# A cross-attention and mixture-of-experts layer on one core: a new order of loads, weight splits and transposes in its first and last stages

## The chip, the cores and the metric

The kernel runs on one NeuronCore of a Trainium2 chip, as one launch. The metric is the device time in microseconds (us) of that launch, median of several runs. A profiled execution gives a trace besides: start and duration of each instruction on the engines PE (TensorE, matrix products), DVE (VectorE), ACT (ScalarE), POOL (GpSimd) and SP (SyncE, which issues most DMAs).

## What is computed

Eight sequences of 112 rows, width 512, go through one layer:

```python
x = x + attention(layernorm(x), ctx)       # q, k_new, v_new = x wq, x wk, x wv
                                           # keys and values: [ctx (375 rows); x (112 rows)], softmax, times wo
x = x + ffn(layernorm(x))                  # 8 experts, the 2 best of each row, weights by softmax over the 2
# expert: y = (silu(x Wg) * (x Wu)) Wd, inner width 1024, everything float32
```

Every product of two float32 matrices is made of three products in a reduced format (fp32r): a = ah + al, b = bh + bl, and ab is taken as ah bh + ah bl + al bh. So each operand has a "hi" part, written by ACT (a copy into fp32r), and a "lo" part, written by DVE (the whole minus hi). PE needs both.

## The kernel before, in words

All engines run a program of their own, written out by hand; they meet only at semaphores, and on each engine the order of the code is the order of the work. The eight sequences go through attention in four pairs (A, B); then come the eight experts, each in eight units of 128 inner columns, in a loop over four pairs of experts.

Names: `x_all` the rows, `mr_all` their mean and 1/std, `xn` normalised rows, `T`, `PJ`, `SC`, `R` the PSUM banks, `xTh/xTl` transposed rows, `wTs/wTh/wTl` a weight as loaded, hi and lo (0 is wq, 1 wk, 2 wv, 3 wo), `qTh/kTh` and their lo parts, `kTs/vs` context keys and values, `vh/vl`, `vnh/vnl` values in parts, `ex` the exponentials, `aTh/aTl` these transposed, `on` the attention output, `oTh/oTl` that transposed, `xr` rows normalised for the experts, `ng` a loaded expert unit, `uh/ul` its parts, `eb` an expert's 256 gathered rows in parts, `gs/us/hs/hf/hh/hl` the hidden layer.

The start. SP issues x of the first two sequences, both halves of wq, x of the next two, then wk, wv, the contexts of pair 0, wo and the rest of x. DVE takes the statistics of a sequence (`stat_x`, `var_x`), POOL the power -0.5 of the variance, DVE normalises (`norm_x`), PE transposes (`pe_xT`), ACT and DVE split the result. Meanwhile ACT and DVE split the weights, in halves of 1024 elements a partition (`hi_w`, `lo_w`), and PE makes four projections (`pe_proj`: two for q, two for k, 24 products each). DVE also takes the statistics of sequences 2 and 3 and normalises them here, between the splits of wq and those of wk. While PE waits for the first data it runs products on the identity whose results nobody reads (`pe_idle`).

A pair (`body`). PE: `pe_vnew` A, `pe_scores` A, `pe_vnew` B, `pe_aT` A (transposes of `ex`), `pe_scores` B, transposes of the next pair's `xn`, `pe_attn` A (12 products), `pe_aT` B, then `pe_attn` B, `pe_oT` A and B, `pe_wo` A and B, with the projections of the next pair in between, and `pe_x2T`. In the last pair there is no next pair, and these stand next to each other. Each transpose is answered by ACT (hi) and DVE (lo) before PE can use it. The values' lo part (`vl`) is made by POOL, three instructions for each sequence (`lo_v`). SP waits for each stage and loads the next pair's contexts.

Towards the experts. SP loads four units in the last pair; ACT and DVE split the first three (`hi_u`, `lo_u` with u = 0, 1, 2). The rows of the first expert are gathered on PE: `pe_early` brings those of the first three pairs, read back from DRAM into `early`, and `pe_pick` those of the last pair. Between them PE runs transposes, logits, the `pe_prefix` products and idle products. `pe_gu_first` makes the first unit's two products; then the loop over units: `pe_gu` of the next unit, at two units of each expert (i == 3 and i == 6) the transposes of the next expert's rows (`pe_eT`, split by `hi_e` and `lo_e`), `pe_down` of the unit before. `pe_eT` for i == 6 waits for the lo part of the one before.

Of the kernel before, what the change touches and what calls it, by code (L numbers as in the profile page):

```python
# [40 lines left out]
def build_kernel(nc, x, ctxT, ctxn, w_all, gwt, units, out):  # L41
# [3 lines left out]
    with stack:  # L45
# [155 lines left out]
        w_hi, w_lo = sem("w_hi"), sem("w_lo")  # L201
        x_stat, x_rstd, x_norm = sem("x_stat"), sem("x_rstd"), sem("x_norm")
# [14 lines left out]
        total, most_ok = sem("total"), sem("most_ok")  # L217
# [6 lines left out]

        def hl_matmul(o, lh, ll, rh, rl, n):
            last = None
            for k in range(n):
                nc.tensor.matmul(o, lh(k), rh(k), start=k == 0, stop=False)  # L228
                nc.tensor.matmul(o, lh(k), rl(k), start=False, stop=False)  # L229
                last = nc.tensor.matmul(o, ll(k), rh(k), start=False, stop=k == n - 1)  # L230
            return last
# [12 lines left out]
        def pe_proj(c, bank):  # L244
# [25 lines left out]
        def pe_attn(pe, g, a, bank):  # L270
# [18 lines left out]
        def pe_wo(pe, g, a, bank):  # L289
            pe.wait_ge(o_lo, g + 1)  # L290
            hl_matmul(bank[0:S, :], lambda k: oTh[a][:, k, :], lambda k: oTl[a][:, k, :],
                      lambda k: wTh[3][:, k, :], lambda k: wTl[3][:, k, :], KT).then_inc(wo_mm, 1)
# [84 lines left out]
        def pe_gu_first(pe):  # L377

            pe.wait_ge(u_lo, 1)
            for w in range(2):  # L380
                for k in range(KT):
                    if w == 0 and k % 2 == 0:
                        pe.wait_ge(e_lo, k // 2 + 1)
                    c = slice(w * D + 128 * k, w * D + 128 * k + 128)
                    last = gu_product(GB[0][w], uh[0][:, c], ul[0][:, c], eb[0], k)
                last.then_inc(gu_mm if w else g_mm, 1)
# [30 lines left out]
        def pe_experts(pe, it, more=True):  # L417


            for u in range(1, UB + 1):  # L420
# [5 lines left out]
                if (i == 3 or i == 6) and (more or e == 0):  # L426
# [10 lines left out]
        def _(pe):  # L437
            pe.wait_ge(ident_ok, 1)
            pe_idle(R, 30)
# [3 lines left out]
            pe.wait_ge(x_lo, 2)  # L443
            pe.wait_ge(w_lo, 1)
            pe_proj(0, SC[0])
# [930 lines left out]
```

## Time and profile before

| | |
|---|---|
| three runs | 462.8, 463.65, 464.78 us (median 463.65) |
| the profiled execution | 463.22 us |
| its span, first to last instruction | 461.4 us |
| PE busy with products | 443.8 us, 96% of the span |
| DVE busy | 346.2 us, 75% |
| ACT busy | 251.7 us, 55% |
| POOL busy | 95.8 us, 21% |
| mean granted TensorE clock | 0.992 of full |
| share of PE in the chain that ended last | 89% |

PE is counted as busy when products run, useful or idle ones. The stage borders, in us from the span's start: the first projections 10 to 22, pair 0 until 67, pair 3 from 135 to 163, the way to the experts until 175, the experts until 452, and the last rows' way to DRAM until the end. Products are pipelined: a row's duration includes its latency, and products in a row start every 0.11 us (224 columns) or 0.23 us (512 columns).

### The profile page before, as it was taken

To read this page: it belongs to the slowest core of one execution; us is meant where nothing else is said; L and a number is where in the kernel's file an instruction comes from. 1 tells how busy PE (TensorE), PEld (TensorE's weight loads), DVE (VectorE), ACT (ScalarE), POOL (GpSimd) and SP (SyncE) were. 2 spreads that over 40 slices of the span, in tenths; PEclk is the share of its full clock that TensorE was granted. 3 is DMA by queue.
4 is the path that set the end of the run, shared out by engine and by line. 5 is a ranking of instruction groups with operands and counts; after the bars stand their busy time and mean duration, and the time that the engine had idled before them with its cause. 6 is when DMAs were issued, how large, how long until landed. Compare 5 with 4: busy or idle time off the path is not lost.

```text
span 461.4 us, 7183 instructions
## 1 busy us (share of the span) xinstructions
PE 443.8 (96%) x2549; PEld 376.0 (82%) x2549; DVE 346.2 (75%) x653; ACT 251.7 (55%) x409; POOL 95.8 (21%) x122
## 2 busy tenths in 40 slices
PE   8899999999999899999999999999999999999991
PEld 6878888888888578888888888888888888888870
DVE  5856646556644577998888888888888888888850
ACT  3648434524533536656656656656656656656621
POOL 4005071552425424003003003003003003003002
PEclk9999999999999999999999999999999999999996
DMA  8975994505544464955956946856856946856203
GB/s 237 396 229 150 290 238 138 167 23 145 195 137 189 123 224 115 344 199 200 268 172 194 277 167 200 270 166 202 269 168 200 276 161 220 264 160 201 40 1 51
DMA packets 26912, 88.40 MB, mean 192 GB/s; under 512 B 2560, under 2 KB 8704, under 8 KB 26880
## 3 DMA queue, kind: packets, MB, share of 16 engines
q1 hardware_dynamic: 23296, 80.13, 53.1%
q0 software_dynamic: 3584, 7.88, 8.3%
q8 instruction: 16, 0.26, 0.2%
q14 instruction: 16, 0.13, 0.1%
HBM read 73.55 MB, written 14.45 MB: 191 GB/s over the span
## 4 chain that ended last, share of the span: by engine, by line
PE 89%; DVE 4%; ACT 2%; POOL 1%; DMA 1%; issue 0%; POOLq 0%; SPq 0%; DVEq 0%; ACTq 0%
PE PJ L340 13%; PE T L340 13%; PE PJ L341 7%; PE T L341 7%; PE SC L228 4%; PE SC L230 4%; PE SC L229 4%; PE SC L413 3%; PE SC L412 3%; PE SC L411 3%; PE PJ L228 3%; PE PJ L230 3%; PE PJ L229 3%; PE T L236 3%; PE R L411 2%; PE R L412 2%
## 5 line engine op out<-in xcount | busy, mean ns | idle before, releaser
L750 DVE TENSOR_TENSOR ul<-ng,uh 128x1536 fp32r<-128x1536 f32 x64 | 112.5, 1758 | 3.1 <-ACT uh L536 2.1
L536 ACT ACTIVATE uh<-ng 128x1536 fp32r<-128x1536 f32 x64 | 94.6, 1480 | 0.0
L340 PE MATMUL PJ<-eb,uh 128*128 128x512 f32 x256 | 91.5, 397 | 0.1
L340 PE MATMUL T<-eb,uh 128*128 128x512 f32 x256 | 91.5, 397 | 0.0
L341 PE MATMUL PJ<-eb,ul 128*128 128x256 f32 x256 | 72.0, 281 | 0.0
L341 PE MATMUL T<-eb,ul 128*128 128x256 f32 x256 | 71.9, 281 | 0.0
L1170 POOL DMA_INDIRECT out<-ys,yidx x16 | 27.8, 1740 | 196.7 <-ACT ys L689 194.3
L340 PEld LDWEIGHTS PJ<-eb,uh 128*128 128x128 f32 x256 | 48.1, 188 | 11.7 <-issue 0.3
L340 PEld LDWEIGHTS T<-eb,uh 128*128 128x128 f32 x256 | 48.1, 188 | 11.5
L341 PEld LDWEIGHTS T<-eb,ul 128*128 128x128 f32 x256 | 48.3, 189 | 1.3
L341 PEld LDWEIGHTS PJ<-eb,ul 128*128 128x128 f32 x256 | 48.3, 189 | 1.3
L228 PE MATMUL SC<-xTh,wTh 128*128 128x224 f32 x128 | 36.0, 281 | 1.6 <-DVE wTl L750 1.0
L1108 POOL TENSOR_TENSOR vl<-vs,vh 128x512 fp32r<-128x512 f32 (+1 forms) x24 | 30.2, 1289 | 27.5 <-ACT vh L536 20.5
L229 PE MATMUL SC<-xTl,wTh 128*128 128x224 f32 x128 | 35.1, 274 | 0.0
L230 PE MATMUL SC<-xTh,wTl 128*128 128x224 f32 x128 | 35.1, 274 | 0.0
L536 ACT ACTIVATE us<-PJ 128x256 f32<-128x256 f32 x32 | 12.3, 384 | 32.6 <-PE PJ L341 32.6
L1013 DVE TENSOR_TENSOR hf<-us,hs 128x256 f32<-128x256 f32 x64 | 27.2, 425 | 2.9 <-ACT hs L699 0.9
L1015 DVE TENSOR_TENSOR hl<-hf,hh 128x256 fp32r<-128x256 f32 x64 | 27.2, 425 | 2.2
L536 ACT ACTIVATE us<-T 128x256 f32<-128x256 f32 x32 | 12.3, 384 | 30.0 <-PE T L341 30.0
L699 ACT ACTIVATE hs<-gs 128x256 f32<-128x256 f32 x64 | 26.3, 411 | 2.4 <-DVE gs L997 2.3
L228 PEld LDWEIGHTS SC<-xTh,wTh 128*128 128x128 f32 x128 | 24.6, 192 | 2.2 <-DVE wTl L750 1.2
L411 PE MATMUL SC<-uh,hh 128*128 128x512 f32 x64 | 25.8, 404 | 0.0
(206 smaller groups left out, 924.6 us busy)
## 6 DMA issues: line engine op xcount, KB each, us to landing
ng<-in_units SPq DMA_DIRECT2D x64, 768.0 KB, 4.3
vs<-in_ctxn SPq DMA_DIRECT2D x8, 768.0 KB, 4.9
kTs<-in_ctxT SPq DMA_DIRECT2D x8, 750.0 KB, 4.9
slots<-zero SPq DMA_DIRECT2D x8, 514.0 KB, 11.6
xe<-slots SPq DMA_DIRECT2D x8, 514.0 KB, 4.3
wTs<-in_weights SPq DMA_DIRECT2D x8, 512.0 KB, 9.4
out<-x_all SPq DMA_DIRECT2D x8, 224.0 KB, 3.7
x_all<-in_x SPq DMA_DIRECT2D x1, 896.0 KB, 18.0
```

What stands on the lines that cost most here:

```text
L228: nc.tensor.matmul(o, lh(k), rh(k), start=k == 0, stop=False)
L229: nc.tensor.matmul(o, lh(k), rl(k), start=False, stop=False)
L230: last = nc.tensor.matmul(o, ll(k), rh(k), start=False, stop=k == n - 1)
L340: nc.tensor.matmul(o[:, :].rearrange("p (h s) -> p h s", h=2), wh, both[:, k, :, :], start=k == 0, stop=False)
L341: return nc.tensor.matmul(o[:, 0:CAP], wl, both[:, k, 0, :], start=False, stop=k == KT - 1)
L411: nc.tensor.matmul(o, hh[b][:, s], wh, start=i == 0, stop=False)
L536: nc.scalar.activation(o, i, ACT.Copy).then_inc(s, 1)
L750: v.tensor_tensor(o, whole, hi.bitcast(F32), ALU.subtract).then_inc(s, 1)
L1013: link(v.tensor_tensor(hf[b][:, :], us[b][:, :], hs[b][:, :], ALU.mult))
L1015: v.tensor_tensor(hl[b][:, :], hf[b][:, :], hh[b][:, :].bitcast(F32), ALU.subtract)\
L1108: g_.tensor_tensor(vl[a][0:n, j, :], vs[a][0:n, j, :], vh[a][0:n, j, :].bitcast(F32), ALU.subtract).then_inc(v_lo, 1)
L1170: pool.indirect_dma_start(out[:, :], bass.IndirectOffsetOnAxis(yidx[:, e, t:t + 1], 0), ys[:, t, :], None, compute_op=ALU.add).then_inc(y_ ...
```

## The change

It has four groups of edits.

At the start: SP issues wk before x of sequences 2 and 3. The variance of each of the two first sequences goes to POOL by itself, and POOL takes two powers of one column in place of one of two. The first half of wq is split in two quarters, 512 elements a partition each (`hi_first_w`, `lo_first_w`), which ACT and DVE do after the split of the matching x; each half of the first projection waits for one quarter. All of wk is split before q is evicted. There is one idle product fewer (29).

In pair 0: statistics and normalising of sequences 2 and 3 now stand in the body, at the places that pairs 1 and 2 have for theirs. ACT copies `vh` of both sequences earlier.

In the last pair: the transposes of `ex` B come amid `pe_attn` A, those of `on` A amid `pe_attn` B, those of `on` B amid `pe_wo` A. ACT and DVE split `on` A's transposes before unit 0, and DVE makes `ul` of unit 1 only after the rows for the first expert.

Towards the experts: 15, 7 and 3 idle products in place of 12, 5 and 8; the two last sums of the counts come after `rows`; `pe_gu_first` opens its bank with a product on zeros and takes the `ul` products as soon as the hi part of the rows is there; the first transposes of the next expert come at i == 4 in place of i == 3; SP issues the loads of units 4 to 6 before those of the gathered rows `xe`.

The start on DVE, before (`wTl_102` is wq's lo part, `wTl_105` that of wk):

```order
L750 TENSOR_TENSOR wTl_102<-wTs_101,wTh_100 128x4x256
L750 TENSOR_TENSOR xTl<-T,xTh 128x4x112 x2
L750 TENSOR_TENSOR wTl_102<-wTs_101,wTh_100 128x4x256
L767 BN_STATS st<-x_all 112x6
L768 BN_AGGR mr_all<-st 112x2
L767 BN_STATS st<-x_all 112x6
L768 BN_AGGR mr_all<-st 112x2
L771 TENSOR_SCALAR ve_all<-mr_all 112x2
L777 TENSOR_SCALAR xn_146<-x_all,mr_all 112x512
L777 TENSOR_SCALAR xn_147<-x_all,mr_all 112x512
L750 TENSOR_TENSOR qTl<-SC,qTh 128x448
L750 TENSOR_TENSOR wTl_105<-wTs_104,wTh_103 128x4x256
```

and the same place after the change:

```order
L781 TENSOR_TENSOR xTl<-T,xTh 128x4x112
L781 TENSOR_TENSOR wTl_102<-wTs_101,wTh_100 128x4x128
L781 TENSOR_TENSOR xTl<-T,xTh 128x4x112
L781 TENSOR_TENSOR wTl_102<-wTs_101,wTh_100 128x4x128
L781 TENSOR_TENSOR wTl_102<-wTs_101,wTh_100 128x4x256
L781 TENSOR_TENSOR wTl_105<-wTs_104,wTh_103 128x4x256 x2
L781 TENSOR_TENSOR qTl<-SC,qTh 128x448
```

The seven instructions of statistics and normalising between wq and wk are gone from here, and both halves of wk stand before the first `qTl`.

The last pair on PE, before (`ex_131` is B's, `on_132` A's and `on_133` B's; the rows begin amid the twelve products of A and leave out what repeats up to B's seventh):

```order
L279 MATMUL PJ<-vh_124,aTh_136 112x512
L280 MATMUL PJ<-vl_122,aTh_136 112x512
L281 MATMUL PJ<-vh_124,aTl_138 112x512
L279 MATMUL PJ<-vh_124,aTh_136 112x512
L280 MATMUL PJ<-vl_122,aTh_136 112x512
L281 MATMUL PJ<-vh_124,aTl_138 112x512
L236 MATMUL T<-ident,ex_131 128x112 x4
L274 MATMUL PJ<-vnh_127,aTh_137 112x512
...
L281 MATMUL PJ<-vh_125,aTl_139 112x512
L236 MATMUL T<-ident,on_132 128x112 x4
L236 MATMUL T<-ident,on_133 128x112 x4
L228 MATMUL PJ<-wTh_109,oTh_140 112x512
```

and after:

```order
L285 MATMUL PJ<-vh_124,aTh_136 112x512
L240 MATMUL T<-ident,ex_131 128x112 x4
L288 MATMUL PJ<-vl_122,aTh_136 112x512
...
L285 MATMUL PJ<-vh_125,aTh_137 112x512
L240 MATMUL T<-ident,on_132 128x112 x4
L288 MATMUL PJ<-vl_123,aTh_137 112x512
...
L229 MATMUL PJ<-wTh_109,oTl_142 112x512
L240 MATMUL T<-ident,on_133 128x112 x4
L227 MATMUL PJ<-wTh_109,oTh_140 112x512
```

Each group of four transposes has moved ahead of five products (`ex` B, `on` A), or behind six (`on` B). The number of instructions is the same.

The lo parts in the last pair and towards the experts on DVE, before (`ul_169`, `ul_170`, `ul_171` are units 0, 1, 2):

```order
L750 TENSOR_TENSOR aTl_139<-T,aTh_137 128x448
L750 TENSOR_TENSOR ul_169<-ng_150,uh_161 128x1536
L750 TENSOR_TENSOR oTl_142<-T,oTh_140 128x448
L750 TENSOR_TENSOR oTl_143<-T,oTh_141 128x448
L750 TENSOR_TENSOR ul_170<-ng_151,uh_162 128x1536
L822 TENSOR_TENSOR x_all<-PJ,x_all 112x512
...
L1039 CAST mosti<-most 112x1
L750 TENSOR_TENSOR ul_171<-ng_152,uh_163 128x1536
L997 TENSOR_TENSOR gs_179<-PJ,gs_179 128x256
```

and after:

```order
L781 TENSOR_TENSOR aTl_139<-T,aTh_137 128x448
L781 TENSOR_TENSOR oTl_142<-T,oTh_140 128x448
L781 TENSOR_TENSOR ul_169<-ng_150,uh_161 128x1536
L781 TENSOR_TENSOR oTl_143<-T,oTh_141 128x448
L859 TENSOR_TENSOR x_all<-PJ,x_all 112x512
...
L1074 CAST mosti<-most 112x1
L781 TENSOR_TENSOR ul_170<-ng_151,uh_162 128x1536
L781 TENSOR_TENSOR ul_171<-ng_152,uh_163 128x1536
L1032 TENSOR_TENSOR gs_179<-PJ,gs_179 128x256
```

`oTl` of A has passed `ul` of unit 0, and `ul` of unit 1 has gone from ahead of the residual sum to right ahead of the first hidden layer's work.

The diff, cut to its core:

```diff
+                if pe:
+                    pe.wait_ge(first_lo, h + 1)
                 last = hl_matmul(bank[:, h * 2 * S:(h + 1) * 2 * S],
...
                 nc.tensor.matmul(o, aTh[a][0:n, j + 1, :], vh[a][0:n, j, :], start=False, stop=False)
+                if amid and j == 1:
+                    amid()
                 nc.tensor.matmul(o, aTh[a][0:n, j + 1, :], vl[a][0:n, j, :], start=False, stop=False)
...
+            for k in range(KT):
+                if amid and k == 2:
+                    amid()
...
             pe.wait_ge(u_lo, 1)
-            for w in range(2):
-                for k in range(KT):
-                    if w == 0 and k % 2 == 0:
-                        pe.wait_ge(e_lo, k // 2 + 1)
...
+            for h in range(2):
+                pe.wait_ge(e_hi, h + 1)
+                for k in (2 * h, 2 * h + 1):
+                    nc.tensor.matmul(GB[0][0][:, 0:CAP], ul[0][:, 128 * k:128 * k + 128], eh[0][:, k, :], start=False, stop=False)
+                pe.wait_ge(e_lo, h + 1)
...
-                if (i == 3 or i == 6) and (more or e == 0):
+                if (i == 4 or i == 6) and (more or e == 0):
...
+                    pe_attn(pe, A, 0, PJ[0], lambda: pe_aT(pe, B, 1, T[0]))
+                    pe_attn(pe, B, 1, PJ[1], lambda: pe_oT(pe, A, 0, T[1]))
+                    pe_wo(pe, A, 0, PJ[0], lambda: pe_oT(pe, B, 1, T[2]))
+                    pe_wo(pe, B, 1, PJ[1])
+                    pe_x2T(pe, A, 0, T[0])
+                    return
...
-            hi_w(0, 0)
             hi_x(0, 0, T[2])
+            hi_first_w(0)
             hi_x(1, 1, T[1])
+            hi_first_w(1)
             hi_w(0, 1)
+            hi_w(1, 0)
+            hi_w(1, 1)
             hi_pj(0, 0, SC[0])
-            hi_w(1, 0)
+            hi_w(2, 0)
...
                     hi_c(1, 1)
+                    hi_v(0, 0)
                 do_exp(A, 0)
...
                 hi_a(A, 0, T[0])
                 if p == 0:
-                    hi_v(0, 0)
+                    hi_v(1, 1)
...
-            g_.tensor_tensor(mr_all[:, 0:2, 1], ve_all[:, 0:2], half[0:S, 0:2], ALU.pow).then_inc(x_rstd, 1)
+            g_.tensor_tensor(mr_all[:, 0:1, 1], ve_all[:, 0:1], half[0:S, 0:1], ALU.pow).then_inc(x_rstd, 1)
+            pool.wait_ge(x_stat, 2)
+            g_.tensor_tensor(mr_all[:, 1:2, 1], ve_all[:, 1:2], half[0:S, 0:1], ALU.pow).then_inc(x_rstd, 1)
...
-            for h in range(2):
-                load_w(0, h)
-            sp.dma_start(x_all[:, 2:4, :], xv[:, 2:4, :]).then_inc(x_in[2], 16)
-            for n in range(1, 3):
+            for n in range(2):
                 for h in range(2):
                     load_w(n, h)
+            sp.dma_start(x_all[:, 2:4, :], xv[:, 2:4, :]).then_inc(x_in[2], 16)
...
-            load_ahead(0, range(2))
+            load_ahead(0, range(LG))
             sp.wait_ge(x2_out, 16 * NB + 16 * 2)
             for a in range(2):
                 sp.wait_ge(scattered[a], 32 * PAIRS)
-            load_xe(0, 0)
             sp.wait_ge(early_T, 1)
             load_xe(ER, 1)
-            load_ahead(0, range(2, LG))
+            load_xe(0, 0)
```

## Rows read from the trace of the kernel before

**Rows 1.** Busy time by stretch: us, then PE, PEld, DVE, ACT, POOL, clock, DMA, GB/s.
```profile
40.00:135.00 95.00, 95.00 (x627) 81.92 (x626) 57.33 (x129) 44.55 (x68) 34.13 (x38) 1.00 0.57 161
192.00:300.00 108.00, 108.00 (x578) 92.39 (x577) 96.79 (x167) 68.22 (x114) 10.85 (x9) 1.00 0.68 217
```

**Rows 2.** Timeline of PE, first projections: start, duration, instruction, [idle before it].
```profile
10.07 0.37 PE L228 MATMUL SC<-xTh,wTh 128*128 128x224 f32 x1 [0.54 <-DVE xTl L750]
...
16.74 0.37 PE L228 MATMUL SC<-xTh,wTh 128*128 128x224 f32 x1 [1.05 <-DVE wTl L750]
...
22.09 0.27 PE L230 MATMUL SC<-xTh,wTl 128*128 128x224 f32 x1
22.52 0.49 PE L228 MATMUL PJ<-wTh,xTh 128*112 128x512 f32 x1 [0.16 <-DVE wTl L750]
```

**Rows 3.** Timelines of ACT and of DVE in the same stretch.
```profile
7.98 0.98 ACT L536 ACTIVATE xTh<-T 128x448 fp32r<-128x448 f32 x2 [0.29 <-PE T L236]
...
14.01 1.00 DVE L777 TENSOR_SCALAR xn<-x_all,mr_all 112x512 f32<-112x512 f32 x2 [0.89 <-POOL mr_all L1113]
```

**Rows 4.** Timeline of PE, `pe_attn` of the first sequence.
```profile
37.38 0.48 PE L279 MATMUL PJ<-vh,aTh 119*112 119x512 f32 x1 [0.30 <-POOL vl L1108]
```

**Rows 5.** Timelines of POOL and DVE where both work; `kTl` subtractions: duration min/median/max.
```profile
38.17 3.79 POOL L1108 TENSOR_TENSOR vl<-vs,vh 128x512 fp32r<-128x512 f32 x3 [0.84 <-ACT vh L536]
...
41.25 2.29 DVE L750 TENSOR_TENSOR kTl<-kTs,kTh 128x1500 fp32r<-128x1500 f32 x1 [1.30 <-ACT kTh L536]
...
98.43 7.53 POOL L1108 TENSOR_TENSOR vl<-vs,vh 128x512 fp32r<-128x512 f32 x6 [2.35 <-DVE xr L832]
...
104.22 0.53 DVE L771 TENSOR_SCALAR ve_all<-mr_all 112x2 f32<-112x2 f32 x1
...
L750 DVE TENSOR_TENSOR kTl<-kTs,kTh x8: 1705/1722/2289, 22.6 to 122.1; 128x1500 fp32r<-128x1500 f32 x8
```

**Rows 6.** Timeline of PE, last pair.
```profile
150.52 0.55 PE L236 MATMUL T<-ident,ex 112*128 112x112 f32 x4
152.35 0.49 PE L274 MATMUL PJ<-vnh,aTh 112*112 112x512 f32 x1 [1.29 <-DVE aTl L750]
...
157.27 0.49 PE L228 MATMUL PJ<-wTh,oTh 128*112 128x512 f32 x1 [0.49 <-DVE oTl L750]
...
163.56 0.60 PE L236 MATMUL T<-ident,xr 112*128 112x112 f32 x4 [0.45 <-DVE xr L832]
```

**Rows 7.** Timelines of DVE and of ACT, last pair.
```profile
152.11 1.49 ACT L536 ACTIVATE uh<-ng 128x1536 fp32r<-128x1536 f32 x1
...
158.77 1.76 DVE L750 TENSOR_TENSOR ul<-ng,uh 128x1536 fp32r<-128x1536 f32 x1 [0.75 <-ACT uh L536]
160.44 0.69 DVE L822 TENSOR_TENSOR x_all<-PJ,x_all 112x512 f32<-112x512 f32 x1
```

**Rows 8.** The tile `early`: its load's issue (first and last start), its landing, its use.
```profile
L1256 SPq DMA_DIRECT2D early<-slots x1: 388/388/388, 158.7 to 158.7; - x1
...
DMA to landing us min/median/max: 3.7/3.7/3.7
...
164.62 2.05 PE L360 MATMUL SC<-ident,early 128*128 128x128 f32 x16
```

**Rows 9.** Timelines of DVE and of PE, first unit of the first expert.
```profile
175.95 1.75 DVE L750 TENSOR_TENSOR ul<-ng,uh 128x1536 fp32r<-128x1536 f32 x1
...
178.76 0.42 DVE L1011 TENSOR_TENSOR us<-PJ,us 128x256 f32<-128x256 f32 x1 [0.73 <-ACT us L536]
...
180.00 0.42 DVE L1015 TENSOR_TENSOR hl<-hf,hh 128x256 fp32r<-128x256 f32 x1
...
180.97 0.40 PE L411 MATMUL SC<-uh,hh 128*128 128x512 f32 x1
```

**Rows 10.** Timelines of PE and of DVE, first transposes of the next expert's rows.
```profile
189.39 0.60 PE L236 MATMUL R<-ident,xe 128*128 128x128 f32 x4
...
194.33 0.68 DVE L750 TENSOR_TENSOR eb<-R,eb 128x512 fp32r<-128x512 f32 x1
```

More of the change, by code:

```diff
@@ L227, in hl_matmul @@
             for k in range(n):
-                nc.tensor.matmul(o, lh(k), rh(k), start=k == 0, stop=False)
-                nc.tensor.matmul(o, lh(k), rl(k), start=False, stop=False)
-                last = nc.tensor.matmul(o, ll(k), rh(k), start=False, stop=k == n - 1)
+                last = hl_matmul_k(o, lh(k), ll(k), rh(k), rl(k), k, n)
             return last
@@ L379, in pe_gu_first @@
             pe.wait_ge(u_lo, 1)
-            for w in range(2):
-                for k in range(KT):
-                    if w == 0 and k % 2 == 0:
-                        pe.wait_ge(e_lo, k // 2 + 1)
-                    c = slice(w * D + 128 * k, w * D + 128 * k + 128)
-                    last = gu_product(GB[0][w], uh[0][:, c], ul[0][:, c], eb[0], k)
-                last.then_inc(gu_mm if w else g_mm, 1)
+            for h in range(2):
[3 more added lines that the diff above has]
+                pe.wait_ge(e_lo, h + 1)
+                for k in (2 * h, 2 * h + 1):
+                    last = nc.tensor.matmul(GB[0][0][:, :].rearrange("p (h s) -> p h s", h=2), uh[0][:, 128 * k:128 * k + 128],
+                                            eb[0][:, k, :, :], start=False, stop=k == KT - 1)
+            last.then_inc(g_mm, 1)
+            for k in range(KT):
+                c = slice(D + 128 * k, D + 128 * k + 128)
+                last = gu_product(GB[0][1], uh[0][:, c], ul[0][:, c], eb[0], k)
+            last.then_inc(gu_mm, 1)
         def pe_gu(pe, it, u):
@@ L478, in body @@
                     pe_xT(pe, A + 3, 1, T[1])
+                if not more:
+                    pe_attn(pe, A, 0, PJ[0], lambda: pe_aT(pe, B, 1, T[0]))
[4 more added lines that the diff above has]
+                    return
                 pe_attn(pe, A, 0, PJ[0])
                 pe_aT(pe, B, 1, T[0])
-                if more:
-                    pe.wait_ge(x_lo, A + 4)
-                    pe_proj(0, SC[0])
-                if p and more:
+                pe.wait_ge(x_lo, A + 4)
+                pe_proj(0, SC[0])
+                if p:
                     pe_prefix(pe, p - 1)
@@ L711, in experts @@
                         hi_u(it + 1, LG)
-                    if (i == 3 or i == 6) and (more or e == 0):
+                    if (i == 4 or i == 6) and (more or e == 0):
                         hi_e(2 * (2 * it + e + 1) + 1 + i // 6, (e + 1) % 2, i // 6, YB[(e + 1) % 2][i // 6])
@@ L851, in topk, with sums @@
                 dve.wait_ge(masked, p + 1)
+                if p < PAIRS - 1:
+                    sums(p)
+            def sums(p):
                 link(v.tensor_tensor(mnew[:, :], mboth[:, 0, :], mboth[:, 1, :], ALU.add))
@@ L931, in body @@
                     x2_norms(A - 1, 1)
-                if p and more:
-                    if p == 1:
-                        dve.wait_ge(x_in[3], 16)
+                if more:
+                    if p < 2:
+                        dve.wait_ge(x_in[2 + p], 16)
                     stat_x(A + 2)
@@ L939, in body @@
                 do_max(A, 0)
-                if p and more:
+                if more:
                     stat_x(A + 3)
@@ L947, in body @@
                 lo_a(A, 0, T[0])
-                if p and more:
+                if more:
                     norm_x(p + 1)
@@ L974, in body @@
                 lo_o(B, 1, T[2])
-                if not more:
-                    lo_u(0, 1)
                 x2_stats(A, 0, PJ[0])
@@ L990, in _ @@
             rows(PAIRS - 1)
+            sums(PAIRS - 1)
             lo_first(0)
@@ L1022, in experts @@
                         sum_g(it + 1, 0)
-                    if (i == 3 or i == 6) and (more or e == 0):
+                    if (i == 4 or i == 6) and (more or e == 0):
                         lo_e(2 * (2 * it + e + 1) + 1 + i // 6, (e + 1) % 2, i // 6, YB[(e + 1) % 2][i // 6])
@@ L1039, in _ @@
             v.tensor_copy(mosti[:, 0:1], most[:, 0:1]).then_inc(most_ok, 1)
-            for u in range(2, LG):
+            for u in range(1, LG):
                 lo_u(0, u)
```

105 lines of the change are left out of this document (55 added, 50 removed).

## The prediction

> **What bounds the kernel now.** I read the busy time by stretch first. From 40 to 135 us PE is busy for 95.00 of 95.00 us and from 192 to 300 for 108.00 of 108.00, at a granted clock of 1.00 [rows 1]. So in three quarters of the span nothing but fewer products could help, and the change takes none away there. What it can win lies where PE waits: the timeline of PE shows waits in the first projections [rows 2], once in the first sequence's attention [rows 4], and in the last pair [rows 6]. Time won in front of such a full stretch goes through it undiminished, since what follows waits for PE. The terms below are therefore differences in the time at which PE reaches a place, and they add.
>
> **The start.** Before, the first projection begins at 10.07 and the first product of `pe_vnew` at 22.52, 12.45 us for 96 products [rows 2]. The last 48 begin between 16.74 and 22.09, that is one each 0.114 us, a slow first one included. Without a gap 96 take about 10.8 us. The gap is 1.65 us, and the wait in it is for wk's lo part, which on DVE stood behind the statistics and the normalising of sequences 2 and 3, whose last piece is the row at 14.01 with 0.89 of idling ahead of it [rows 3]. After the change both halves of wk are split before `qTl`. My count of DVE from the split of x on: half a wq (1.2 us) and two of wk (2.3 us) are over at about 14.4, wanted at 15.8 and later; it holds as long as wk has landed by about 12, and its loads now stand ahead of a 448 KB load. I take the whole 1.65.
> Against it stands a later begin. The transposes are there at 7.98 and ACT splits the two x in 0.98 us [rows 3]. Now a quarter of wq stands between the two on ACT (0.6 us by my estimate, 512 elements against 448 in 0.5) and one on DVE (0.7); before, the first half of wq filled the time until 7.98 and was no burden. I get xTl at 10.25 in place of 10.0: 0.2 us lost (0 to 0.5). The earlier variance of x 0 buys nothing, as PE runs idle products until 7.3 anyway; the one dropped idle product gives 0.1, counted in. Net 1.45 us (bounds 0.8 to 1.8).
>
> **Pair 0.** PE waits 0.30 us at 37.38 for POOL's last piece of `vl`, with the slower restart 0.4 us [rows 4]. ACT's copy of `vh` moves ahead of the first exponential, where ACT idles, so POOL can begin earlier. But POOL's program has the power for sequences 2 and 3 first, and this now waits for DVE's statistics in the body. I put the begin of `vl` at 30.4 against 33.5; all three pieces at 34.2, wanted after 35. Gain 0.4 (0 to 0.5).
> The price: the normalising of sequences 2 and 3, at about 31.3 in the new time, now lies beside `vl` on POOL, which it did not in any pair before. The trace shows what such company does. A subtraction of two SBUF tensors that usually takes 1.72 took 2.29 when it began at 41.25 while POOL worked until 41.96; and the `ve_all` at 104.22, a two-element operation, took 0.53 and ended where the fifth of POOL's six pieces of 1.25 us (from 98.43) ends [rows 5]. DVE seems to be held until POOL's instruction in flight is over. For the two `xn` no row exists. Below: 0, if they slip in between. Above: each held a whole piece, so that the second ends about 1.1 us after PE wants its transpose at 32.9. I take one of them held for one piece, nearest to the row at 104.22: 0.6 us lost on PE (0 to 1.1).
> The Trainium skill, GPSIMD Engine Reference, section Specifications, says that GpSimd shares its SBUF interfaces with VectorE, with contention for instructions in a 2-port mode or with two SBUF inputs. The rows at 41.25 and 104.22 agree. By this rule the `xn` are exposed if they run in a 2-port mode, and the loss is in the upper half of the range; if they don't, it is 0 and the sum is better by 0.6.
>
> **The last pair.** In the old time scale. The transposes of `ex` B begin at 150.52 and the product that needs their lo part at 152.35: 1.83 us for transposes, ACT, DVE [rows 6]. They now begin five products of 0.233 us earlier, at 149.35 (the exponential is over at about 149.25, so with no reserve). The product starts at 151.2, 1.17 us earlier, 0.3 of it still a wait. `on` A's transposes come after seven of its twelve products, at 152.9, and with the same 1.83 us `pe_wo` A can begin at 154.7 in place of 157.27 [rows 6]. `on` B's transposes stand in the middle of it and cost it 0.4 us; they need ACT's scaling, which stands behind the copy of unit 0, an operation of 1.49 us [rows 7], and is done at about 156.0, where PE arrives at 156.15. `pe_wo` A ends 2.2 us earlier. On DVE the residual sum A began at 160.44, held by `ul` of unit 1 (158.77, 1.76 us) and not by PE [rows 7]; that `ul` is gone from there, and `ul` of unit 0 and `oTl` B are over at about 158.0. So sum, statistics and `x2T` A come 2.25 us earlier, at 161.3 in place of 163.56. I take 2.25 (bounds 1.6 to 2.5).
>
> **To the experts.** `early` is issued at 158.7 and takes 3.7, so it is there at 162.4; PE used it at 164.62 [rows 8], 2.2 us of slack. POOL's scatters ahead of it don't move with this pair's edits, so the slack is used up: PE arrives at 162.4 too. Besides, the store of `x_all` A is now issued beside it. I take 0.15 lost (0 to 0.7). The sums moved behind `rows` give 0.1; the idle products (25 after the last transposes before and after) only shift.
> `ul` of unit 1, one more operation like that at 175.95, now stands ahead of the first hidden layer: 1.67 us more on DVE. There, 0.73 us were idle at 178.76, and the chain ended at 180.42 with `pe_down` at 180.97 [rows 9]. I count `hl` ready at 181.42, so `pe_down` starts 0.5 us late (0.2 to 0.9). The `ul` products of unit 0 ahead of the wait for the lo part make PE about 0.24 us earlier at the unit's end, but only to wait longer for DVE: worth nothing. From then on DVE recovers, because it needs less than PE for a unit, and a backlog in the loop costs nothing. The move from i == 3 to i == 4 adds nothing to either engine.
>
> **The sum.** 1.45 + 0.4 - 0.6 + 2.25 - 0.15 + 0.1 - 0.5 = 2.95 us. The profiled execution took 463.22 us, a span of 461.4 and 1.8 around it; with the change 460.3. The median of the runs lies 0.43 higher, at 463.65: 460.7 us.
>
> **Rivals.** (1) The waits come back: the `xn` held for all of 1.1 us, `early` 0.7, `pe_down` 0.9, wk landing somewhat late. The sum falls by 1.45 to 1.5: 462.1. For it: three terms have no slack in my count, and a place where PE arrives just in time is usually late. Against it: each has been counted with durations of the trace. (2) The company on POOL does nothing and the start is not later: 2.95 + 0.6 + 0.3, time 459.8. For it: `ve_all` is a poor guide to a long operation. (3) Slower than before: the expert loop. `pe_eT` at i == 6 waits for the lo part of the transposes before, which now are two units ahead, not three. Before, transposes at 189.39 had their lo part at 195.01, 5.6 us [rows 10]. A unit lasts 4.2 us, so 8.4 are left. The point is 8.4 us from transposes to lo part; if the chain took 9.4, seven experts would lose 1 us each, 7 in all, time 467.7. Against it: 2.8 us of slack. (4) The change doesn't do what it says at the start (wk late from DRAM) and gives all of 1.45 back, with the loss of 0.6: 462.2 at best, and with rivals' losses no difference, 463.
>
> **How the numbers follow.** A change under 0.5%, 2.3 us, can't be told from none in this kernel; faster begins at 461.3. Chances: forecast 46%, its own range 459.9 to 461.5; rival 2 20%; rival 1 26%; rival 4 4%; rival 3 4%. Faster: nearly all of the forecast, rival 2 and a little of rival 1, 0.67. Same 0.29, slower 0.04. The range runs from 459.2, all gains at their better bound but one, to 462.7, beyond rivals 1 and 4.
>
> **What would show it.** In the new profile: no wait of PE between the first projection and `pe_vnew`, and these 10.8 us apart; no wait on `vl`; `xn` of 2 and 3 longer than 0.55 us or begun late, and a wait of PE on `xn` around 32.9; in the last pair `x2T` A 161.3 - 1.25 = 160.1 or so in the new scale; a wait of PE on `early`; a wait on `hl` of about 0.75 us at the first `pe_down`; full PE in the loop. The forecast is wrong if any of the last pair's transposes waits more than 0.5 us, if wk's split waits for its load beyond 15, or if PE shows waits in the loop.

## The result: slower, and where the trace shows it

The changed kernel took 467.82 us (median of 5 runs, 467.44 to 468.62), the kernel before 464.69 (5 runs in all): ratio 1.0082, 95% interval 1.0058 to 1.0106. It is slower by 0.8%, some 3.8 us by this ratio (3.1 by the two medians), where the forecast was 460.7. The profiled execution took 468.43 us with a span of 466.7, against 463.22 and 461.4.

I read the waits of PE first. In this view a row names the waiting engine, tile and line, what it waited for, the us in total, how often and the longest:

```profile
PE T L240 <- DVE xn L814: 5.4, 1, 5.4
PE R L357 <- POOL ident L1097: 1.6, 1, 1.6
PE SC L227 <- DVE xTl L781: 0.8, 1, 0.8
PE R L429 <- DVE hl L1050: 0.8, 1, 0.8
PE SC L429 <- DVE hl L1050: 0.7, 1, 0.7
PE SC L227 <- DVE qTl L781: 0.6, 2, 0.4
PE T L240 <- DVE xr L869: 0.2, 1, 0.2
PE SC L371 <- DMA early<-slots: 0.2, 1, 0.2
```

The waits in the last pair [rows 6] and the one on `vl` [rows 4] are gone. One new wait of 5.4 us outweighs them all. The timelines of PE, DVE and POOL around it:

```profile
33.20 0.39 PE L229 MATMUL SC<-kTh,qTl 128*112 128x488 f32 x1
39.01 1.76 PE L240 MATMUL T<-ident,xn 112*128 112x112 f32 x8 [5.43 <-DVE xn L814]
40.45 0.75 PE L280 MATMUL PJ<-vnh,aTh 112*112 112x512 f32 x1
40.99 0.63 PE L281 MATMUL PJ<-vnl,aTh 112*112 112x512 f32 x1
41.42 0.63 PE L282 MATMUL PJ<-vnh,aTl 112*112 112x512 f32 x1
...
44.52 0.40 PE L288 MATMUL PJ<-vl,aTh 119*112 119x512 f32 x1
44.75 0.40 PE L289 MATMUL PJ<-vh,aTl 119*112 119x512 f32 x1
```

```profile
31.73 0.61 DVE L781 TENSOR_TENSOR aTl<-T,aTh 128x448 fp32r<-128x448 f32 x1
32.25 6.70 DVE L814 TENSOR_SCALAR xn<-x_all,mr_all 112x512 f32<-112x512 f32 x1
```

```profile
31.23 5.00 POOL L1145 TENSOR_TENSOR vl<-vs,vh 128x512 fp32r<-128x512 f32 x4
34.97 3.71 POOL L1145 TENSOR_TENSOR vl<-vs,vh 128x512 fp32r<-128x512 f32 x3
```

The first `xn` lasts 6.70 us; alone it takes 0.54. It ends at 38.95, when POOL's six pieces of `vl` (31.23 to 38.68, one every 1.24) are over; a piece is one of the instructions that make `vl`, three for each sequence. Beside it `aTl`, with one operand in PSUM, took its usual 0.6. PE stands still from 33.58 to 39.01 and then starts 512-column products every 0.43 us, not every 0.23. The windows say why (us, then busy us of PE, PEld, DVE, ACT and POOL, the granted clock, DMA share, GB/s):

```profile
34.00:36.00 2.00, 0.00 (x0) 0.00 (x0) 2.00 (x1) 0.00 (x0) 2.00 (x2) 1.00 0.52 137
36.00:38.00 2.00, 0.00 (x0) 0.00 (x0) 2.00 (x1) 0.00 (x0) 2.00 (x3) 0.82 0.72 259
38.00:40.00 2.00, 0.99 (x5) 0.99 (x6) 1.99 (x3) 0.00 (x0) 0.67 (x1) 0.50 0.00 0
40.00:42.00 2.00, 2.00 (x9) 1.63 (x8) 0.72 (x3) 1.62 (x4) 0.00 (x0) 0.50 0.03 8
42.00:44.00 2.00, 2.00 (x7) 1.38 (x6) 0.65 (x3) 0.00 (x0) 0.00 (x0) 0.50 0.00 0
44.00:46.00 2.00, 2.00 (x15) 1.73 (x14) 0.00 (x0) 0.43 (x1) 0.00 (x0) 0.97 0.00 0
```

While PE idles its clock falls from 2.4 to 1.2 GHz (1.00 to 0.50), and it stays low for some 5 us more under full work. The wait is paid for twice.

The other borders of the forecast in the timeline of PE of the changed kernel, to be held against [rows 2, 6, 8, 9]:

```profile
10.16 0.37 PE L227 MATMUL SC<-xTh,wTh 128*128 128x224 f32 x1 [0.80 <-DVE xTl L781]
...
16.17 0.34 PE L227 MATMUL SC<-xTh,wTh 128*128 128x224 f32 x1 [0.39 <-DVE qTl L781]
...
19.28 0.34 PE L227 MATMUL SC<-xTh,wTh 128*128 128x224 f32 x1 [0.20 <-DVE qTl L781]
...
22.03 0.39 PE L227 MATMUL PJ<-wTh,xTh 128*112 128x512 f32 x1
...
45.30 0.35 PE L227 MATMUL SC<-xTh,wTh 128*128 128x224 f32 x1
...
168.15 0.60 PE L240 MATMUL T<-ident,xr 112*128 112x112 f32 x4 [0.20 <-DVE xr L869]
...
169.45 2.05 PE L371 MATMUL SC<-ident,early 128*128 128x128 f32 x16 [0.16 <-DMA early<-slots]
...
186.16 0.50 PE L429 MATMUL SC<-uh,hh 128*128 128x512 f32 x1 [0.69 <-DVE hl L1050]
...
455.34 0.50 PE L429 MATMUL R<-uh,hh 128*128 128x512 f32 x1 [0.80 <-DVE hl L1050]
```

The same five borders in every profile, as the stretch from one to the next (us, subtracted from such rows). A: span's start to the first product of `pe_vnew`. B: to the first projection of pair 1. C: to `x2T` A of the last pair. D: to the first down product. E: to the last product that waits for `hl`. "Median" and "ratio" come from the timed runs, the ratio against the kernel before on the same chip, whose own median was between 463.80 and 464.69 us.

| kernel | A | B | C | D | E | median | ratio (95%) |
|---|---|---|---|---|---|---|---|
| before | 22.52 | 15.96 | 125.08 | 17.41 | 269.08 | 463.80 to 464.69 | |
| changed | 22.03 | 23.27 | 122.85 | 18.01 | 269.18 | 467.82 | 1.0082 (1.0058 to 1.0106) |
| norms_then_vl | 21.91 | 16.25 | 123.58 | 20.56 | 269.17 | 461.86 | 0.9947 (0.9931 to 0.9963) |
| gap_after_three | 21.86 | 18.90 | 123.17 | 18.68 | 269.18 | 463.50 | 0.9984 (0.9959 to 1.0008) |
| norm_two_tensors | 21.50 | 22.72 | 122.96 | 18.69 | 269.20 | 469.01 | 1.0117 (1.0076 to 1.0157) |
| idle_products | 21.41 | 21.00 | 122.90 | 18.38 | 269.19 | 466.20 | 1.0047 (1.0025 to 1.0069) |
| drained_pieces | 21.90 | 15.84 | 122.88 | 18.47 | 269.15 | 460.43 | 0.9919 (0.9897 to 0.9942) |
| vh_back | 21.34 | 16.03 | 122.87 | 18.34 | 269.16 | 460.71 | 0.9931 (0.9909 to 0.9952) |
| last_pair_only | 23.84 | 15.95 | 122.89 | 18.46 | 269.17 | 463.07 | 0.9987 (0.9966 to 1.0009) |
| start_only | 21.53 | 16.02 | 125.09 | 17.42 | 269.06 | 462.00 | 0.9955 (0.9940 to 0.9970) |
| ul_in_gap | 21.62 | 15.83 | 122.90 | 17.14 | 268.97 | 459.56 | 0.9901 (0.9881 to 0.9922) |
| ul_in_gap_idle_ahead | 22.21 | 15.80 | 122.87 | 17.18 | 269.07 | 459.56 | 0.9897 (0.9876 to 0.9917) |

The C of norms_then_vl holds a wait of 0.45 us on `xr` in pair 1 that no other profile has. Changed against before: -0.49 + 7.31 - 2.23 + 0.60 + 0.10 = 5.29 us, which is the whole difference of the two spans (5.3). The loss is all in B. In the timed runs the difference is 3.8 us by the ratio and 3.1 by the medians; the profiled execution of before was on the quick side, that of the changed kernel on the slow side.

### The profile page after: what moved, and what is told of

It reads as the page before. It is cut to its first block, busy times and chain, and to the rows that moved or that the text cites. A ratio compares the mean times of both kernels' runs of the same rounds, so it can differ in the third digit from the quotient of the medians.

```text
span 466.7 us, 7187 instructions
## 1 busy us (share of the span) xinstructions
PE 446.4 (96%) x2549; PEld 377.3 (81%) x2549; DVE 351.7 (75%) x655; ACT 252.1 (54%) x410; POOL 96.6 (21%) x123
## 4 chain that ended last, share of the span: by engine, by line
PE 86%; DMA 4%; DVE 4%; issue 1%; SPq 1%; POOL 1%; ACT 1%; POOLq 0%; DVEq 0%; ACTq 0%
PE PJ L351 12%; PE T L351 12%; PE PJ L352 6%; PE T L352 6%; PE SC L227 4%; PE SC L229 4%; PE SC L228 4%; PE SC L429 3%; PE SC L430 3%; PE SC L431 3%; PE PJ L229 3%; PE PJ L227 3%; PE PJ L228 3%; PE T L240 3%; DMA wTs<-in_weights 2%; PE R L429 2%
## 5 line engine op out<-in xcount | busy, mean ns | idle before, releaser
L351 PE MATMUL PJ<-eb,uh 128*128 128x512 f32 x252 | 90.1, 397 | 0.0
L352 PE MATMUL PJ<-eb,ul 128*128 128x256 f32 x252 | 70.8, 281 | 0.0
```

Source lines behind the costliest of these rows:

```text
L351: nc.tensor.matmul(o[:, :].rearrange("p (h s) -> p h s", h=2), wh, both[:, k, :, :], start=k == 0, stop=False)
L352: return nc.tensor.matmul(o[:, 0:CAP], wl, both[:, k, 0, :], start=False, stop=k == KT - 1)
```

## Experiments

My theory after this comparison: VectorE's `xn` can't start as long as POOL runs its `vl` pieces back to back, and the clock falls behind it. Rivals: `xn` is late for a reason of its own, the move of the normalising costs by itself, or the slow products have another cause.

**Normalise first (norms_then_vl).**

```diff
                 if p == 0:
+                    pool.wait_ge(x_norm, 4)
                     lo_v(0, 0)
                     lo_v(1, 1)
```

> The changed kernel, but POOL waits for both xn of sequences 2 and 3 before it begins the six pieces of vl in pair 0. Theory A (VectorE's xn can't start while POOL works through its pieces back to back, and the products behind it then run at half clock): xn take 0.55 us each again, PE's wait of 5.43 us on xn shrinks to 0.2 to 0.6, vl ends at about 37.6 and costs PE 0.3 to 0.9 in attention A, the half clock around 38 to 44 is gone (2.3 us); net 6 to 7.5 us less than the changed kernel, about 461. Theory B (xn was late for a reason of its own, its statistics or its power coming late, and the company of vl only took one piece's time): the wait on xn stays at 4 us or more and the time stays above 466.

B falls by 7.02 us to 16.25, and the kernel is faster than the one before by 0.5%. Timeline of DVE:

```profile
32.14 0.99 DVE L814 TENSOR_SCALAR xn<-x_all,mr_all 112x512 f32<-112x512 f32 x2
```

Both `xn` take 0.99. So they were ready to run at 32.1 and, in the changed kernel, were held by POOL; theory B has fallen.

**A pause after three pieces (gap_after_three).**

```diff
                     lo_v(0, 0)
+                    pool.wait_ge(x_norm, 4)
                     lo_v(1, 1)
```

> The changed kernel, but POOL waits for both xn after its first three pieces of vl (sequence 0), before the other three. Theory A1 (xn is held until POOL has nothing to run, a pause anywhere lets it through): first xn begins when the third piece ends, about 34.97, ends by 35.3, second by 35.8; PE waits about 2 us on xn instead of 5.43; half clock gone or shorter; 4 to 6 us less than the changed kernel, about 463. Theory A2 (xn is held for a fixed time or until a certain piece of six, whatever POOL does next): the wait stays at 5.43 or xn ends before 34.9.

Timelines of DVE and of POOL:

```profile
32.09 3.49 DVE L814 TENSOR_SCALAR xn<-x_all,mr_all 112x512 f32<-112x512 f32 x2
```

```profile
31.07 3.78 POOL L1145 TENSOR_TENSOR vl<-vs,vh 128x512 fp32r<-128x512 f32 x3
35.66 1.28 POOL L1145 TENSOR_TENSOR vl<-vs,vh 128x512 fp32r<-128x512 f32 x1 [0.82 <-DVE xn L814]
```

POOL's third piece ends at 34.85; the two `xn` end at 35.58. The longest `xn` is 3.04 us. The hold ends with POOL's run of pieces, after three here as after six before. PE waited 1.76 us. That wait too was enough for the clock: it was at 0.95, 0.50 and 0.69 in the three windows from 34 to 40, and of the 2.94 us that B is longer than before the wait explains only 1.4 (1.76 less the 0.4 that `vl` cost). The rest lies with the half clock; it was not measured apart here. The timed runs can't be told from the kernel before.

**The shortest pause (drained_pieces).**

```diff
                     g_.tensor_tensor(vl[a][0:n, j, :], vs[a][0:n, j, :], vh[a][0:n, j, :].bitcast(F32),
                                      ALU.subtract).then_inc(v_lo, 1)
+                    if g < 2:
+                        pool.wait_ge(v_lo, 3 * g + j + 1)
```

> The changed kernel, but in pair 0 POOL waits after each piece of vl until that piece has completed before it issues the next: the same six pieces, with a short pause after each and no wait on VectorE. Theory A1 (xn is let through at the first pause of POOL, however short): first xn, issued at about 32.2, ends by 33.0 and the second by 33.5 to 34.5; PE waits 0.2 to 1.2 us on it instead of 5.43, the clock stays at 1.00; 5.5 to 7 us less than the changed kernel, 461 to 462.5. Theory A3 (a pause must be long, near the 0.8 us that POOL stood still after three pieces, or all six pieces must be over): xn still ends at about 39 and the time is 467.8 or more.

Timelines of DVE (the second `xn`) and of POOL:

```profile
32.63 1.50 DVE L814 TENSOR_SCALAR xn<-x_all,mr_all 112x512 f32<-112x512 f32 x1
34.05 0.65 DVE L842 TENSOR_REDUCE mx<-SC 112x1 f32<-112x487 f32 x1
```

```profile
31.11 5.53 POOL L1145 TENSOR_TENSOR vl<-vs,vh 128x512 fp32r<-128x512 f32 x4
35.34 4.04 POOL L1145 TENSOR_TENSOR vl<-vs,vh 128x512 fp32r<-128x512 f32 x3
```

A POOL that waits for the end of its own piece before it issues the next loses about 0.15 us a piece (1.40 apart, not 1.24), and lets `xn` through: the first wasn't held, the second for one piece. The two cases start alike: the first `xn` was issued 1.03 us after the first piece began here, and 1.02 us after it in the changed kernel. PE waits 0.34 on it and never on `vl`. B is 15.84, the kernel 460.43 us, 0.8% faster than before. One waiting instruction a piece turns the change from a loss into a gain.

**Undo one edit (vh_back).** ACT's copies of `vh` go back to their old places.

```diff
                     hi_c(1, 1)
-                    hi_v(0, 0)
                 do_exp(A, 0)
...
                 hi_a(A, 0, T[0])
                 if p == 0:
-                    hi_v(1, 1)
+                    hi_v(0, 0)
...
                     hi_x(A + 3, 1, T[1])
+                if p == 0:
+                    hi_v(1, 1)
```

> The changed kernel with one edit undone: ACT's copies of vh in pair 0 stand again behind the split of aT (sequence 0) and behind those of xT (sequence 1), so that POOL's vl begins at about 33.0 and not at 31.2. Theory A (the overlap in time of xn with the run of vl is the whole loss): xn take 1.0 us for both, at most the second is held behind one or more pieces; PE waits at most 0.5 on xn and 0.3 to 0.5 on vl; 461 to 462, 6 to 7 us less than the changed kernel. Theory B (moving the normalising behind the scores is itself what costs, by its statistics and power): a wait on xn of over 4 us stays and the time stays above 466.

460.71 us, B 16.03 with the old wait of 0.30 on `vl`. So the edit that I booked as a gain of 0.4 us, the earlier `vh`, is what pushed POOL's run onto `xn`. The moved normalising costs nothing by itself.

**Which operations are held (norm_two_tensors, vl_by_copy, other_operations).** Three edits of the changed kernel, all in pair 0: the first two in place of `xn`'s and `vl`'s operation, the third ahead of both `xn`.

```diff
+                        v.scalar_tensor_tensor(xn[a][:, :], x_all[:, b, :], mr_all[:, b, 0:1],
+                                               mr_all[:, b, 1:2].to_broadcast([S, D]),
+                                               ALU.subtract, ALU.mult).then_inc(x_norm, 1)
```
```diff
+                        g_.tensor_copy(vl[a][0:n, j, :], vs[a][0:n, j, :]).then_inc(v_lo, 1)
```
```diff
+                    link(v.reduce_max(mx[:, 1, :], x_all[:, 2, :], AX.X))
+                    link(v.tensor_scalar(R[0:S, :], x_all[:, 2, :], mr_all[:, 2, 0:1], mr_all[:, 2, 1:2],
+                                    ALU.subtract, ALU.mult))
```

> The changed kernel, but the two xn of pair 0 are computed by scalar_tensor_tensor, whose second operand is 1/sigma broadcast along the row, a form with two tensors read from SBUF instead of one tensor and two scalars; POOL's vl as in the changed kernel. Theory A (only an operation with one tensor input in the fast mode needs the port that POOL holds; one with two tensor inputs is interleaved with POOL, as kTl was with 2.29 us for 1.72): each xn takes 0.6 to 1.2 us beside vl, PE waits 0.3 to 1.5 on xn, time about 461 to 463. Theory B (any operation of VectorE with SBUF operands is held as long as POOL runs back to back): the wait of 5.4 us stays and the time is that of the changed kernel, 467.8.

> The changed kernel, but POOL's six pieces in pair 0 are copies of vs, an operation with one input tensor, instead of the subtraction with two (the lo part of v is therefore wrong in pair 0). Theory E1 (any run of POOL with SBUF operands holds VectorE's xn): xn ends when the six copies are over, however long these take. Theory E2 (only POOL's form with two input tensors does): xn take 1.0 us for both and PE's wait on xn is under 1 us.

> The changed kernel with two more operations on VectorE in pair 0 right ahead of xn, beside POOL's vl: a maximum over 512 SBUF elements per partition (one input, one element out), and the same normalising written to PSUM instead of SBUF. Theory F1 (held are only operations that have both input and output in SBUF in the fast form or two SBUF inputs): both take about 0.6 to 0.7 us beside vl, as bn_stats did with 0.69 in the kernel before, and the first xn behind them is held until the six pieces are over, about 39. Theory F2 (tensor_scalar is held whatever it writes to): the one that writes PSUM takes until about 38.9, and xn behind it 0.5 each.

With two tensors from SBUF (the tile `xn`; durations min, median, max in ns):

```profile
L815 DVE SCALAR_TENSOR_TENSOR xn<-x_all,mr_all x2: 740/3740/6739, 31.9 to 38.6; 112x512 f32<-112x512 f32 x2
```

Theory A of that run has fallen: this form is held for 6.74 us as well. I had taken `kTl`'s 2.29 [rows 5] for sharing; by its times it was a hold too. It began at 41.25, POOL's third piece ended at 41.96, and what is left after that, 1.58, is nearly the 1.72 of the operation alone.

With copies on POOL (timelines of DVE, first the one `xn`, then both, and of POOL):

```profile
32.12 0.98 DVE L814 TENSOR_SCALAR xn<-x_all,mr_all 112x512 f32<-112x512 f32 x1
...
32.12 1.73 DVE L814 TENSOR_SCALAR xn<-x_all,mr_all 112x512 f32<-112x512 f32 x2
```

```profile
31.08 3.80 POOL L1146 CAST vl<-vs 128x512 fp32r<-128x512 f32 x6
```

Six copies, also back to back, held the first `xn` 0.44 us and both together 0.74, and both were over at 33.85, a microsecond before the copies. Neither E1 nor a pure E2: copies hold for part of one instruction, and the subtractions keep VectorE out from piece to piece. The copies differ from them in two things, the single input and the length (0.61 to 0.80 us each, a subtraction 1.27 or more), and which of the two ends the long hold isn't shown. The one run of this kernel took 460.11 us.

With other operations on DVE beside the `vl` of the changed kernel:

```profile
32.71 0.68 DVE L813 TENSOR_REDUCE mx<-x_all 112x1 f32<-112x512 f32 x1
33.42 0.81 DVE L814 TENSOR_SCALAR R<-x_all,mr_all 112x512 f32<-112x512 f32 x1
34.27 5.14 DVE L819 TENSOR_SCALAR xn<-x_all,mr_all 112x512 f32<-112x512 f32 x1
```

The maximum over SBUF and the normalising into PSUM ran through; the same normalising into SBUF, next in line, took 5.14 us. F1 holds. (One run of this kernel, 468.87 us.)

One held operation does not fit a hold until the run is over (timelines of POOL and of DVE in the changed kernel, pair 1):

```profile
67.52 7.52 POOL L1145 TENSOR_TENSOR vl<-vs,vh 128x512 fp32r<-128x512 f32 x6 [2.35 <-DVE xr L869]
73.31 0.53 DVE L807 TENSOR_SCALAR ve_all<-mr_all 112x2 f32<-112x2 f32 x1
```

This `ve_all` of two elements takes 0.17 us when POOL is idle. Here it was held and ended at 73.84, while the sixth piece of the same run, begun at 73.78, lasted until 75.04. It did so in the kernel before too, at 104.22 [rows 5]. So a small operation got past between two back-to-back pieces, and the `xn` did not. No run here shows why.

The Trainium skill says nearly this of the operations that are held. "SBUF — State Buffer", section "SBUF: two separate sides", makes the port pair of VectorE and GpSimd an exclusive lock, held for a whole instruction, which a VectorE operation wants in a 2-port mode or with two SBUF inputs, the latter only against a GpSimd operation that reads SBUF. "VectorE: DVE Perf Modes", section "What auto-detection actually checks", gives such a mode to a single source and a destination both in SBUF, if their outermost sizes are both even or are equal. The rows agree on which operations are held: `xn` 6.70 and 6.74 us, the two others 0.68 and 0.81. On how long, they show more than that: a lock held for one instruction would be 1.24 us, and the `xn` was kept out for up to six instructions in a row, which the sections cited don't speak of.

**The clock (idle_products).**

```diff
+                if p == 0:
+                    pe_idle(R, 48)
                 if more:
                     pe_xT(pe, A + 2, 0, T[2])
```

> The changed kernel with 48 idle products of 256 bf16 columns (about 0.107 us each, 5.1 us) on PE between the scores of sequence 1 and the transposes of xn in pair 0, where PE waits anyway. Theory A (PE's idling in front makes the clock fall, which then costs a second time): xn still ends at about 38.95, but the 8 transposes take 0.93 instead of 1.76 us and the first 512-column products follow each other by 0.23 instead of 0.43 us; 2.3 us less than the changed kernel, 465.5. Theory B (the slow products come from something else, such as POOL or VectorE traffic): granted clock and spacing stay as they were, 467.8 or more.

Windows of this kernel, columns as above:

```profile
36.00:38.00 2.00, 2.00 (x21) 1.73 (x18) 2.00 (x1) 0.00 (x0) 2.00 (x2) 1.00 0.42 156
38.00:40.00 2.00, 1.82 (x14) 1.36 (x12) 1.52 (x4) 0.41 (x1) 0.06 (x1) 1.00 0.00 0
40.00:42.00 2.00, 2.00 (x10) 1.54 (x9) 1.18 (x3) 1.22 (x4) 0.00 (x0) 1.00 0.00 0
```

The clock stays at 1.00, the eight transposes take 1.06 us and products start every 0.23. `xn` is held as before (6.71). B falls from 23.27 to 21.00: 2.27 us of the loss are the clock, the other 5.04 are the wait, less the 0.4 that `vl` no longer costs.

**Parts of the change alone (last_pair_only, start_only).** Each is the kernel before with one group of edits; `start_only` also moves statistics and normalising into pair 0 but leaves `vh` where it was. last_pair_only also has all edits from the first unit on; the core of its diff:

```diff
+                    pe_attn(pe, A, 0, PJ[0], lambda: pe_aT(pe, B, 1, T[0]))
+                    pe_attn(pe, B, 1, PJ[1], lambda: pe_oT(pe, A, 0, T[1]))
+                    pe_wo(pe, A, 0, PJ[0], lambda: pe_oT(pe, B, 1, T[2]))
...
+                    hi_o(A, 0, T[1])
                     hi_u(0, 0)
...
-                if not more:
-                    lo_u(0, 1)
```

And of the second:

```diff
-            for h in range(2):
-                load_w(0, h)
-            sp.dma_start(x_all[:, 2:4, :], xv[:, 2:4, :]).then_inc(x_in[2], 16)
-            for n in range(1, 3):
+            for n in range(2):
                 for h in range(2):
                     load_w(n, h)
+            sp.dma_start(x_all[:, 2:4, :], xv[:, 2:4, :]).then_inc(x_in[2], 16)
...
-                if p and more:
+                if more:
                     norm_x(p + 1)
```

> The kernel before with only the last pair's and the experts' edits (transposes amid products, the deferred copy and lo part of units, the early loads of units, the sums moved, the first unit's order, i == 4). My term of the forecast, 2.25 gained, less 0.15 on early, less 0.5 at the first down product, plus 0.1: 1.7 us less than before, ratio 0.9963; all waits up to 140 us as before. Rival: most of it is lost again at early and at the first down product, because loads and VectorE's lo part can't follow: less than 0.7 us.

> The kernel before with only the start's edits: x alone at the queue's head, the first half of wq in two quarters, wk ahead of sequences 2 and 3, their statistics and normalising in pair 0; vh and vl of pair 0 where they stood before. Forecast's term as first put: 1.45 less than before. What the changed kernel showed: wk lands late (its split waits 1.1 and 1.4 us on ACT), so that only 0.5 to 0.6 is left, ratio 0.9988 or 463.6; xn not held or only the second, by up to 1.2 us, since vl begins at about 33. If xn is held as in the changed kernel: 5 us more than before.

C is 122.89 with the last pair's edits and 125.09 without: 2.2 us gained. D grows from 17.41 to 18.46, so 1.1 is left, and the timed difference is 0.13% with an interval across zero (its ten runs lie between 461.5 and 465.2). `start_only` gave 0.45% (0.30 to 0.60), 2.1 us, more than either number I had written down. Neither has the loss of B.

**What the last pair gives back (ul_in_gap, ul_in_gap_idle_ahead).** Both on top of drained_pieces.

```diff
             lo_lr(1)
+            lo_u(0, 1)
             topk(PAIRS - 1)
...
-            for u in range(1, LG):
+            for u in range(2, LG):
                 lo_u(0, u)
```
```diff
             pe_early(pe, SC)
-            pe_idle(T[2], 4)
...
+            pe_idle(T[2], 5)
             pe.wait_ge(early_in, 16)
```

> The kernel with drained pieces, and VectorE's lo part of unit 1 moved from behind the first experts' sums to behind the lo parts of xr, ahead of the last routing, where VectorE idled 1.96 us waiting for the logits (the lo part takes 1.75). Theory C (that lo part, put in front of the first hidden layer by the change, is what makes the first down product wait 0.72 us): the wait falls to 0.1 or less, routing begins no later than before by more than 0.1; 0.6 us less than with drained pieces alone (460.4), so 459.8. Rival: the wait stays, since the first hidden layer waits for silu on ACT anyway; no difference.

> As the kernel with unit 1's lo part in the gap, and in addition the 4 idle products behind the early transposes moved ahead of the wait for early's load, now 5. Theory D (PE's idling of 0.5 to 1.1 us at early, right behind another wait on xr, sometimes takes the clock to a half for 4 us, as in the profile of the kernel that let the norms go first; the 4 idle products behind it only delay the last transposes by 0.43 us): no more wait of over 0.7 us without PE work ahead of it, last transposes 0.4 us earlier, spread of the runs not above 1.5 us; 0.4 to 0.8 us less, 459.2. Rival: the last transposes then wait for xr or the routing for VectorE's lo part, which now stands ahead of it, and nothing is gained.

With unit 1's lo part in a gap of DVE where it waited for the logits, the wait at the first down product is gone, D is 17.14 and the kernel takes 459.56 us: the fastest, 1.0% below the one before and about 8 us below the changed one. Moving the idle products brought nothing more (D 17.18). The last transposes came 0.27 us earlier behind `x2T` A (3.41 us, not 3.68), but routing on DVE did not (5.85 and 5.86): in both kernels it begins where the lo part of unit 1 ends. That was the rival.

Why they were tried is seen in the profile of norms_then_vl, whose D is 20.56. There PE waited twice in short order, the second time 1.09 us on `early`:

```profile
162.00:164.00 2.00, 0.91 (x7) 0.28 (x5) 1.31 (x4) 0.89 (x2) 0.51 (x1) 1.00 0.98 369
164.00:166.00 2.00, 2.00 (x12) 2.00 (x13) 1.83 (x3) 0.63 (x1) 0.57 (x2) 0.67 1.11 355
166.00:168.00 2.00, 2.00 (x12) 1.75 (x11) 0.01 (x1) 0.00 (x0) 0.00 (x0) 0.50 0.85 316
```

`early` then took 3.15 us instead of 2.05. Whether that is also what spreads the runs of last_pair_only was not profiled and stays open.

## Why the prediction was wrong

**The step that failed** is the price of the moved normalising: "I take one of them held for one piece, nearest to the row at 104.22: 0.6 us lost on PE (0 to 1.1)". The mechanism, VectorE held by POOL, was named and is right. Its length was not. I bounded it above by one piece of 1.25 us for each `xn`, because the only held operation that I had read ended at the border of a piece. The runs show 6.70 us for the first `xn`, the whole of POOL's run that lay ahead. Behind it came a cost that I had not considered at all, 2.27 us of half clock. Together B lost 7.31 us where I had +0.2 (0.6 lost, 0.4 gained). The rows that I had could not settle it. `kTl` at 41.25 [rows 5] began in the last piece of a run of three, where the end of the piece and the end of the run are the same. `ve_all` at 104.22, which I took as the nearest, has two elements and did get past between two pieces; the `xn` has 512 and did not. The unsettled point deserved a rival of its own, a hold until the end of the run; there was none.

**The edit that triggers it** was booked on the other side, as the 0.4 us of an earlier `vl`. I worked out both times, `vl` from 30.4 and `xn` at 31.3, and still took the two edits as separate terms. vh_back shows that without the first the second costs nothing.

**The start**: 1.45 forecast, 0.49 in the profile of the changed kernel. The split of wk waited for its load (ACT 1.25 and 1.62 us, the second until 16.28), the point that I had made the term depend on, and past the 15 that I had named as a sign of being wrong. PE still waited 0.39 and 0.20 us between the projections, where I had no wait. But the profiles of one kernel differ here by more than the term: with the start's edits A is 21.34 to 22.48 in twelve profiles, mean 21.8; without them it was 22.52 and 23.84 in two. The timed start_only gained 2.1 us (1.4 to 2.8). The forecast lies just inside; the composition was wrong: the first projection begins no later than before (9.33 to 10.60 against 10.07 and 11.33), and the stretch from there to `pe_vnew` shrinks by about 0.5 us only, where I had 1.65.

**The last pair**: 2.25 forecast, 2.23 measured in C. **To the experts**: -0.15 + 0.1 - 0.5 forecast, so 0.55 lost; D lost 0.60, and 0.93 to 1.35 in most other profiles with these edits: PE waited 0.5 to 0.9 us on `early` in them and 0.16 here. It landed 4.0 to 4.6 us after its issue, 3.7 before. **The wait on `vl`** fell as forecast. **The loop**: nothing, rival 3 did not happen.

Without the failed step the sum would have come out well: vh_back, the change less one edit, took 460.71 us, against 460.7 predicted for the whole. Part of that is luck, as two errors cancel: start_only gained 2.1 us where the sum had 1.45, and last_pair_only 0.6 (from 1.6 gained to 0.4 lost) where it had 1.7. The range failed since its bound for the unknown cost was taken from what one row of a tiny operation showed, not from how long the other engine stayed busy.

## What to carry to other kernels

Before an operation of VectorE is moved beside work of POOL, lay both timelines over each other and look at how long POOL's run of two-input operations is, not at one instruction of it; take all that is left of the run as the upper bound of the hold. Where they must overlap, let POOL wait for its own last instruction between pieces, or put the run behind the operation. And where the change may give PE a new wait of the length of those that took the clock down here (1.09, 1.76 and 5.43 us), add the half clock behind it to the upper bound, or fill the wait with idle products, which brought back 2.27 us here.

## What I had not expected of the hardware

- A VectorE operation of 0.54 us takes 6.70 beside six consecutive two-input subtractions of POOL. With a pause of some 0.15 us between them it takes 0.54, and beside six back-to-back copies 0.98. A two-element operation was held too, but got past between two subtractions.
- A VectorE operation on 512 SBUF elements a partition that writes one element or PSUM is not held (0.68 and 0.81 us), the same arithmetic into SBUF is (5.14).
- A wait of PE of 1.76 us took the clock to 0.50, and so did 1.09 us behind a stretch of little work; in other profiles PE waited up to 0.93 us at the same place and the clock stayed at 1.00. The length of the wait alone doesn't decide: the clock also stayed at 1.00 around waits of 1.29 us (before, at 152.35 [rows 6]) and 1.53 us, here in last_pair_only (timeline of PE, then the window, columns as above):

```profile
11.33 0.37 PE L226 MATMUL SC<-xTh,wTh 128*128 128x224 f32 x1 [1.53 <-DVE xTl L774]
```

```profile
10.00:12.00 2.00, 0.67 (x6) 0.67 (x7) 2.00 (x4) 1.06 (x1) 0.00 (x0) 1.00 1.10 332
```
